# One spill block in DRAM for a tile of eight heads, stacked by reads of 4 KB rows, with heads dealt to tiles by parity

## The reference

```python
xn = adaln(x, cond, ln1_w, ln1_b)               # layernorm, then scale and shift from cond
q, k, v = split(xn @ qkv_w.T)                   # heads of 32 features
q, k = rope(q), rope(k)                         # t1*cos - t2*sin, t2*cos + t1*sin; t1, t2: halves of a head
x = x + attn(q, k, v) @ sa_out_w.T              # softmax(q k^T / sqrt(32)) v
xn = adaln(x, cond, ln2_w, ln2_b)
q = rope(xn @ q_w.T); k = rope(ctx @ k_w.T); v = ctx @ v_w.T
x = x + attn(q, k, v) @ ca_out_w.T
xn = adaln(x, cond, ln3_w, ln3_b)
x = x + gelu(xn @ ffn_w1.T + ffn_b1) @ ffn_w2.T + ffn_b2
```

## Time and profile before

| | |
|---|---|
| median of 3 runs | 1929.85 us (1921.75 to 1933.32) |
| the profiled execution | 1925.28 us, span 1923.5 us |
| PE busy | 1869.4 us, 97% of the span, mean granted clock 0.994 |
| ACT busy | 1383.3 us, 72% |
| DVE busy | 1294.9 us, 67% |
| POOL busy | 785.8 us, 41% |
| DMA | 308.37 MB, mean 160 GB/s |

### The profile page before, as it was taken

The page is one execution under the profiler, slowest core; times in us unless marked ns, Lnnn a source line. Parts: engine busy times, 40 slices in busy tenths (PEclk is TensorE's granted clock), DMA queues, the critical chain, the costliest instruction groups (busy, mean ns, idle before and its releaser), DMA issues. The chain is left out here.

```text
span 1923.5 us, 39339 instructions
## 1 busy us (share of the span) xinstructions
PE 1869.4 (97%) x13460; PEld 1630.4 (85%) x13460; DVE 1294.9 (67%) x2250; ACT 1383.3 (72%) x3813; POOL 785.8 (41%) x818
## 2 busy tenths in 40 slices
PE   8899999999998999999999998899999999999999
PEld 7788888888877888888888886688898998989898
DVE  7766676767776677676776776446667666666754
ACT  4777777888876888888888888655666666565654
POOL 3534433443442454454454441013536354444531
PEclk9999999999998999999999999999999999999999
DMA  7666676566576778767668677343232322323130
GB/s 232 195 203 185 204 223 194 177 200 198 165 220 189 204 212 233 201 197 227 199 200 225 198 217 190 109 137 110 78 99 67 99 88 89 95 71 110 45 99 33
DMA packets 306451, 308.37 MB, mean 160 GB/s; under 512 B 21072, under 2 KB 260048, under 8 KB 306256
## 3 DMA queue, kind: packets, MB, share of 16 engines
q1 hardware_dynamic: 304528, 304.47, 53.4%
q10 hardware_dynamic: 1728, 1.39, 0.3%
HBM read 212.46 MB, written 92.27 MB: 158 GB/s over the span
## 5 line engine op out<-in xcount | busy, mean ns | idle before, releaser
L744 ACT ACTIVATE ps_s<-ps_s,neg_max 128x256 f32<-128x256 f32 x1024 | 452.8, 443 | 55.4 <-DVE neg_max L861 48.3
L861 DVE TENSOR_REDUCE neg_max<-ps_s 128x2 f32<-128x512 f32 x512 | 349.3, 687 | 212.8 <-PE ps_s L615 212.4
L758 ACT ACTIVATE prob<-ps_s 128x512 f32<-128x512 f32 x512 | 303.4, 593 | 137.2 <-PE ps_s L634 134.3
L634 PE MATMUL ps_s<-qT,kT 98*128 98x256 f32 x1024 | 211.6, 289 | 24.4 <-DMA qT<-max_rows 21.8
L931 POOL TENSOR_TENSOR rope_c<-rope_c,rope_s 128x256 f32<-128x256 f32 x128 | 98.4, 769 | 330.5 <-DVE rope_s L836 330.5
L615 PE MATMUL ps_s<-kT,qT 96*128 96x256 f32 x1024 | 216.5, 293 | 10.7 <-ACT ps_s L744 8.3
L615 PEld LDWEIGHTS ps_s<-kT,qT 96*128 96x128 f32 x1024 | 169.9, 190 | 60.3 <-ACT ps_s L744 28.4
L605 PE MATMUL ps_g<-xx_hi,w_hi 128*128 128x256 f32 x1024 | 208.1, 285 | 1.4 <-issue 1.4
L634 PEld LDWEIGHTS ps_s<-qT,kT 98*128 98x128 f32 x1024 | 169.3, 191 | 46.9 <-issue 21.0
L744 ACT ACTIVATION_READ_ACCUMULATOR ps_s<-ps_s,neg_max 128x1 f32 x1024 | 207.8, 203 | 0.0
L605 PE MATMUL ps_g<-xx_lo,w_hi 128*128 128x256 f32 x1024 | 205.5, 282 | 0.0
(11 more groups left out here) (155 smaller groups left out, 4654.7 us busy)
## 6 DMA issues: line engine op xcount, KB each, us to landing
kT<-k_turned SPq DMA_DIRECT2D x384, 128.0 KB, 3.1
qT<-q_turned SPq DMA_DIRECT2D x128, 256.0 KB, 3.9
f_raw<-in_w1T SPq DMA_DIRECT2D x124, 256.0 KB, 3.1
k_turned<-rot_hi SPq DMA_DIRECT2D x64, 256.0 KB, 3.2
k_turned<-rot_lo SPq DMA_DIRECT2D x64, 256.0 KB, 2.5
q_turned<-rot_hi SPq DMA_DIRECT2D x64, 256.0 KB, 3.6
q_turned<-rot_lo SPq DMA_DIRECT2D x64, 256.0 KB, 4.1
qT<-q_turned SPq DMA_DIRECT2D x128, 128.0 KB, 3.9
```

Of the source, the lines that this page charges most:

```text
L634: ins = eng.matmul(ps_s[:, score_bank(step), t * L:(t + 1) * L], kT[:, quad % NQ, j, t * P:(t + 1) * P], qT[:, quad % NQ, j, :], start=Tru ...
L744: ins = eng.activation(scores[:, t * L:(t + 1) * L], scores[:, t * L:(t + 1) * L], ACT.Exp, bias=neg_max[G % 2][:, t, j:j + 1], accum_out= ...
L758: eng.activation(prob[:, n % NP, :, :].rearrange("p t l -> p (t l)"), ps_s[:, score_bank(step), :], ACT.Exp).then_inc(exp_done, 1)
L861: eng.tensor_reduce(neg_max[G % 2][:, :, j], ps_s[:, score_bank(step), :].rearrange("p (t l) -> p t l", l=L), AX.X, ALU.max, negate=True). ...
```

## The change

1. The heads of a tile. Before, tile t holds heads 8t to 8t+7. After, it holds the heads of parity t, and within a tile the partition is (feature, head) with the head innermost, where it was (head, feature). The weight columns are written by `by_halves` in that order: its last dimension now steps over 8 elements (32 bytes), where it ran over 16 contiguous ones. The rope tables repeat each frequency for eight partitions.
2. The DRAM layout. `turned` is (2, tile, part, feature, head, token). One spill DMA fills one whole block of 256 KB; a feature's rows of eight heads are 8 KB in a row.
3. The stacks. One DMA moves 64 rows of 4 KB (high and low), a second 32 rows of 4 KB (high), for k as for q. For k there are two DMAs where there were three. q is stacked as hi, hi, lo, k as hi, lo, hi.
4. The head number n now counts even heads, then odd ones. `mix` takes its columns of v from `feature_of(n)`, and the output weight rows are loaded to match, each row block by four DMAs of 32 rows where there was one of 128.

PE's, DVE's, ACT's and POOL's instructions are as many as before and stand in the same order. Its core:

```diff
+    def feature_of(n):
+        return (T * (n % HG) + n // HG) * HD
...
-        slot_loads[slot] += 1
+        slot_loads[slot] += OH if step[0] == "w_load" and step[2] == "o" else 1
...
-        turned = {m: nc.dram_tensor(f"{m}_turned", (2, D, 2, L), F32, kind="Internal").ap() for m in "qk"}
+        turned = {m: nc.dram_tensor(f"{m}_turned", (2, T, 2, HD, HG, L), F32, kind="Internal").ap() for m in "qk"}
...
-            STACKS = {"q": 2, "k": 3}
+            STACKS = {"q": 2, "k": 2}
...
-                return w[:, row, :].rearrange("p (s h d) -> p h s d", s=2, d=HALF)
+                return w[:, row, :].rearrange("p (u d h) -> p h u d", u=2 * T, d=HALF)
...
-                                ins = eng.matmul(ps_g[:, b, s * L:(s + 1) * L], w[:, row, (T * s + t) * P:(T * s + t + 1) * P], a[:, c, :],
+                                ins = eng.matmul(ps_g[:, b, s * L:(s + 1) * L], w[:, row, (2 * t + s) * P:(2 * t + s + 1) * P], a[:, c, :],
...
-                                                     v_sb[i % NV][:, k, c * P + j * HD:c * P + (j + 1) * HD],
+                                                     v_sb[i % NV][:, k, feature_of(n % H):feature_of(n % H) + HD],
...
+                        elif m == "o":
+                            for j in range(OH):
+                                first = feature_of(OH * c + j)
+                                eng.dma_start(w_raw[j * HD:(j + 1) * HD, slot, :],
+                                              attnT[layer, MATS.index(m), first:first + HD, :]).then_inc(raw_in[slot], 16)
...
-                        out_to = turned[m][i % 2, T * t * P:T * (t + 1) * P].rearrange("(p d) s l -> s p d l", d=2)
+                        high, low = (turned[m][i % 2, t, part].rearrange("(s d) h l -> (d h) s l", s=2) for part in range(2))
...
-                        if m == "q":
-                            eng.dma_start(qT[0:2 * HD, quad % NQ, :, :].bitcast(F32),
-                                          heads.rearrange("(h d) s l -> (d s) h l", d=HD)).then_inc(stack_in[m][n], 16)
-                            eng.dma_start(qT[2 * HD:ROWS, quad % NQ, :, :].bitcast(F32),
-                                          heads[:, 0].rearrange("(h d) l -> d h l", d=HD)).then_inc(stack_in[m][n], 16)
-                        else:
-                            for s in range(2):
-                                eng.dma_start(kT[s:2 * HD:2, quad % NQ, :, :].bitcast(F32),
-                                              heads[:, 0].rearrange("(h d) l -> d h l", d=HD)).then_inc(stack_in[m][n], 16)
-                            eng.dma_start(kT[2 * HD:ROWS, quad % NQ, :, :].bitcast(F32),
-                                          heads[:, 1].rearrange("(h d) l -> d h l", d=HD)).then_inc(stack_in[m][n], 16)
+                        both = turned[m][i % 2, n // 2, :, :, first:first + OH, :].rearrange("s d j l -> (s d) (j l)")
+                        into = (qT if m == "q" else kT)[:, quad % NQ, :, :].rearrange("p h l -> p (h l)").bitcast(F32)
+                        pair, once = (slice(HD, ROWS), slice(0, HD)) if m == "q" else (slice(0, 2 * HD), slice(2 * HD, ROWS))
+                        eng.dma_start(into[pair, :], both).then_inc(stack_in[m][n], 16)
+                        eng.dma_start(into[once, :], both[0:HD, :]).then_inc(stack_in[m][n], 16)
...
-    ang = np.arange(length, dtype=np.float32)[None, :] * np.tile(inv_freq, P // half)[:, None]
+    ang = np.arange(length, dtype=np.float32)[None, :] * np.repeat(inv_freq, P // half)[:, None]
```

More of the change, by code:

```diff
@@ L991, in attention_sync @@
                                 eng.wait_ge(stack_in[m][quad], 16 * STACKS[m] * (i - 1))
-                        out_to = turned[m][i % 2, T * t * P:T * (t + 1) * P].rearrange("(p d) s l -> s p d l", d=2)
+                        high, low = (turned[m][i % 2, t, part].rearrange("(s d) h l -> (d h) s l", s=2) for part in range(2))
                         eng.wait_ge(rot_hi_done, n)
-                        eng.dma_start(out_to[0], rot_hi[:, n % NT, :, :].bitcast(F32)).then_inc(spilled[m][t], 16)
+                        eng.dma_start(high, rot_hi[:, n % NT, :, :].bitcast(F32)).then_inc(spilled[m][t], 16)
                         eng.wait_ge(rot_lo_done, n)
-                        eng.dma_start(out_to[1], rot_lo[:, n % NT, :, :].bitcast(F32)).then_inc(spilled[m][t], 16)
+                        eng.dma_start(low, rot_lo[:, n % NT, :, :].bitcast(F32)).then_inc(spilled[m][t], 16)
                     elif kind == "b1_load":
@@ L1004, in attention_sync @@
                             eng.wait_ge(weigh_done, OH * (quad - NQ + 1))
-                        heads = turned[m][i % 2][n * OH * HD:(n + 1) * OH * HD]
-                        if m == "q":
-                            eng.dma_start(qT[0:2 * HD, quad % NQ, :, :].bitcast(F32),
-                                          heads.rearrange("(h d) s l -> (d s) h l", d=HD)).then_inc(stack_in[m][n], 16)
-                            eng.dma_start(qT[2 * HD:ROWS, quad % NQ, :, :].bitcast(F32),
-                                          heads[:, 0].rearrange("(h d) l -> d h l", d=HD)).then_inc(stack_in[m][n], 16)
-                        else:
-                            for s in range(2):
-                                eng.dma_start(kT[s:2 * HD:2, quad % NQ, :, :].bitcast(F32),
-                                              heads[:, 0].rearrange("(h d) l -> d h l", d=HD)).then_inc(stack_in[m][n], 16)
-                            eng.dma_start(kT[2 * HD:ROWS, quad % NQ, :, :].bitcast(F32),
-                                          heads[:, 1].rearrange("(h d) l -> d h l", d=HD)).then_inc(stack_in[m][n], 16)
+                        first = n % 2 * OH
+                        both = turned[m][i % 2, n // 2, :, :, first:first + OH, :].rearrange("s d j l -> (s d) (j l)")
[3 more added lines that the diff above has]
+                        eng.dma_start(into[once, :], both[0:HD, :]).then_inc(stack_in[m][n], 16)
                     elif kind == "res_load":
```

## The result

| | before | after |
|---|---|---|
| median of the runs | 1929.46 us (9 runs) | 1937.77 us (9 runs, 1931.95 to 1944.91) |
| ratio | | 1.0048, interval 1.0034 to 1.0063 |
| the profiled execution | 1925.28 us, span 1923.5 us | 1941.72 us, span 1939.9 us |
| PE's mean granted clock in it | 0.994 | 0.987 |

The same kernel beside the last set of experiments gave 1.0039 (1.0025 to 1.0053). So the change costs 0.4 to 0.5%, some 8 us. That is within 1%, where the forecast put 0.73. It lies in the wide range (1905 to 1942 us), but outside the forecast's own (1914 to 1930), and it has the other sign: 0.4% faster was forecast. The profiled execution is 4 us above its median, so its rows show somewhat more of the loss than the typical run has. One run of e5, at 4334 us, was disturbed and counts in no ratio.

A forecast was written before the change was run, and what follows sets the result against it. PE was taken as the bound, idle only 54.1 us, with max_rows its largest wait. Terms -6.5 - 1.7 - 1.0 + 1.5 + 0.5 = -7.2 us gave 1918.1 profiled, 1922.6 against the median; own range 1914 to 1930, wide 1905 to 1942.

The forecast's parts named there:

- The weights' stride: Writing q and k weight rows with a 32-byte step delays the start: +0.5 us, bounds nothing to 4.1 us.
- the step costs 14%: Slowdown assumed for strided q and k weight writes, derived from DVE's strided PSUM reduction at L806.
- L821 and L677 stay under 0.8 us: Sign that the weight term is right: the rows at these lines, writing q and k weights, stay this short.
- rival D: Strided q and k weight writes double in time: +3.6 us on the forecast, 1926 us; 0.17 together with B.
- Output rows: Four DMAs per output weight row, 24 more issues, delay ACT in layer 0: +1.5 us, bounds 0 and 2.6.
- `max_rows`: PE's 14 waits for the DMA laying max_rows into qT, 21.8 us, shorten with the backlog ahead: -6.5 us.
- Together `max_rows` lands 0 to 0.9 us sooner where it is late; I take 0.5: Fewer k issues (0 to 0.6 us) plus 4 KB rows (0.3 us) shorten the backlog before late max_rows transfers.
- The clock: One of two max_rows waits, 2.41 and 2.31 us, no longer slows PE's clock: -1.7 us (0 to 3.3).
- The change of layers: Backlog with weight rows between layers shortens alike; two ACT waits for a row shrink 0.5 us each: -1.0 us.
- A: Backlog before max_rows clears in nearly all groups: 1903 us, or 1910 in part; chance 0.17 in full or part.
- B: Nothing but noise: SP's saving lost to waiting on weigh, DMA time per byte unchanged; 1930 us; 0.17 with D.
- C: max_rows rows take turns with 4 KB stack rows, landing 1.2 to 1.4 us later: 1955 us, half 1942; chance 0.14.

The follow-up runs named there:

- e5: Kernel after, with the 64 rows of a k stack read by two DMAs of 32 rows, three DMAs a k quad again: 1932.95 us, ratio 1.0009.
- e1: Kernel after, with q and k weight columns put in the tile's order on the host, so split writes are contiguous: 1933.45 us, ratio 1.0022.
- e2: Kernel after, with output weight rows put in order on the host and each row block loaded by one DMA: 1932.62 us, ratio 1.0008.
- e6: Kernel after, with only the lnT loads (adaptive layernorm weights) placed later, away from max_rows: 1924.36 us, ratio 0.9969.
- e3: Kernel after, with q/k weight columns and output weight rows both ordered on the host, one DMA per row block: 1929.72 us, ratio 1.0001.
- e13: e3 with the lnT loads placed later; an added wait on the residual's load moved nothing: 1917.57 us, ratio 0.9956.
- e14: Kernel before the change, with the lnT loads placed later; an added wait on the residual's load moved nothing: 1924.67 us, ratio 0.9988.
- e11: e3 with token rows padded in DRAM, so stacks move 1 KB pieces in the same two DMAs a quad: 1926.53 us, ratio 1.0000.
- e4: Kernel after, with token rows padded by 512 bytes in DRAM, so stacks move 1 KB pieces in the same DMAs: 1932.71 us, ratio 1.0016.

## Why the prediction was wrong

**The weights' stride: mis-sized, +0.5 for 3.5 us.** "the step costs 14%" failed. It was taken from a reduction that reads PSUM with a step; the writes to SBUF 32 bytes apart take ACT from 634 to 1250 ns and DVE from 680 to 1174. The signal "L821 and L677 stay under 0.8 us" is plainly wrong, the upper bound of 4.1 us nearly right, and rival D's +3.6 us with it; e1, where `max_rows` is issued 3.5 us sooner, shows the cause. The sum also counted DVE's six rows alone; ACT writes the same ones, and no term was made for them. The Trainium skill (SBUF — State Buffer, section Door 1: The DMA port swizzle) has 16-byte cachelines with a penalty for each new one. By that rule the term lay near the doubling; the trace agrees, and the nearest row misled.

**Output rows: +1.5 forecast, 1.9 measured to the second group; right in size, wrong in path.** ACT's first wait is 3.36 us as foretold (3.6), but e2 has the same 3.35 with one DMA a row. The cost sits at the second pair, where SP has issued sixteen loads instead of four. The price of an issue was low as well: eight take 4.08 and 5.15 us, 0.51 to 0.64 each, where I took 0.43.

**`max_rows`: -6.5 forecast, -1.6 in the total, and the clock worse.** The mechanism, that a wait is as long as the backlog ahead, holds; e6 shows it most clearly. The step that failed is "Together `max_rows` lands 0 to 0.9 us sooner where it is late; I take 0.5", applied to every wait alike. In the four lnT groups it landed 0.2, 2.2, 2.0 and 1.8 us later after its issue, and the waits there grew from 4.1 us to 10.2, and 7.5 in the other profile. The two parts of the step were read about right (SP's stretch is 0.8 us shorter, a 4 KB row some 10 to 30 ns less than four of 1 KB), but where `lnT` loads stand in the queue both work the other way: they come closer behind `max_rows`, and its rows wait among longer ones. One example stood for fourteen waits with different queues. In all other groups the forecast held in direction: the waits fell from 17.7 us to 10.0 and 12.6. Part of that is time which the added costs took instead, since without them it is 14.3 (e3). The three terms of the stacks (`max_rows`, clock, change of layers) were put at -9.2 us together; with the lnT loads moved, e13 against e14 is -6 to -7.

**The clock: -1.7 forecast, about +7.** Over the runs, (1 - clock) x span is 13.7 us before (13.0 and 13.6 in the two other sets) and 20.7 after, 19.2 in the second measurement: 6 to 7 of the 8 us, as an estimate, since it also counts slow clock in which PE was idle. I counted a wait that drops out of the slow clock, and none that goes in. The idle time in the lnT groups comes in pieces of 2 to 3 us, and in 5 us behind them the granted clock was 0.84, 0.50, 0.80 and 0.50; before the change the same places are at 1.00. e3 is back at 13.7 us, and e13 at 10.9.

**The change of layers: -1.0 forecast.** PE's wait for `max_rows` there went from 2.83 to 4.18 us. No experiment is about it alone.

**The rivals.** A didn't come. B's result came for the stacks alone (e3, 1.0001), but not for its reason: the table has losses and gains of 3 to 10 us in e3's profile, which in the runs' median cancel. C foresaw that longer rows can delay `max_rows`, and 4 KB rows do so in four groups, in two of them by strung-out rows of about the size it gave; but not wherever a stack is moving: in the other groups waits shortened. For C the prediction names the Trainium skill (DMA: Bandwidth & Descriptors, section Queues, rings and completion order), whose packets hold some 9 to 17 descriptors, where C gave each row a turn; the pauses inside the 16 rows of G8 are nearer to C's. D was right in kind. What no rival had is that the same change shortens one set of waits and lengthens another. (Two of the prediction's sums are off without effect: -2 to -15 us gives 1915 to 1928 us for its own range, and B's +2 - 1 gives 1931.)

**What stays open.** Why the first row of `max_rows` starts later in the lnT groups, and how much of the rest is row length and how much the closer issues. The lnT waits are 5.1 and 6.8 us with 1 KB rows in two DMAs (e11, e4), 8.2 with 4 KB rows and three for k (e5), and 7.5 to 10.4 with both, so each seems to have a share, but single profiles differ by up to 2.6 us. The DMA engines are at 0.99 there, and the records don't say on which engine a row ran. Open too is why e4 and e5, each with both added costs, are at 1.0016 and 1.0009 and not nearer to after. Shifts of 1 us change which groups wait, and the measured 0.4% is made of such things as much as of fixed costs.

## What to carry to other kernels

When a small late transfer shares the DMA engines with others, list what stands ahead of it in each of its waits, not in one; a change of the common part says nothing about the groups with extra loads, and moving those loads (0.9969 with the change in place) was worth more than the whole layout change. When an edit is to move a transfer, look in the trace whether it moved: the residual's here didn't. Read the nearest row of the same memory and the same direction for a strided access: a read of PSUM says nothing about a write of SBUF. Before a kernel is judged by such a change, take out its side costs and the neighbour's loads once: the layout here is +0.4% as it came, 0 without the side costs, and -0.3% with the lnT loads moved in both kernels.

## What the runs showed of the hardware

- Writes of 512 float32 to SBUF with a step of 32 bytes take ACT 1250 ns for 634 and DVE 1174 for 680, while DVE's strided read of 256 elements of PSUM is at 425 ns.
- The median DMA row took 27, 46, 84 and 174 ns for 512 bytes, 1, 2 and 4 KB; by the share of busy stretches the first three are 28, 57 and 106. A share lower by 2.5 points (53.7 to 51.2%) on a kernel whose PE waits for DMAs made no difference in time (e11 against e3).
- A 16-row DMA on ACT's queue had its first row start 1.3 us after the issue and was through at 1.75 us in the median group; with SP's queue full, in G8 after, it was 2.9 and 4.9 us.
- A stack's 64-partition issue takes SP 0.46 to 0.51 us, one of 32 partitions 0.58, and a quarter of a weight row 0.51 to 0.64, no less than a whole one (0.45 to 0.69 in e2).
- A second DMA of a few KB isn't free: splitting a 16-row transfer in two cost 0.45 to 0.54% against the kernel after, and 1.1 us in each quiet transfer (e9).
